# A square on VectorE, a bf16 maximum in a buffer of its own: adaLN block with linear attention and an int8 feed-forward

## The reference

```python
mod = (silu(c) @ wmod).reshape(8, 6, 1, -1)       # sa, ca, ga, sb, cb, gb
ga, gb = (2*(g >= 0) - 1) * max(abs(g), 0.25)     # for both
h = layernorm(x) * (1 + ca) + sa
q, k = relu(h Wq^T) / 8, relu(h Wk^T) / 8         # 16 heads of 64
v, u = h Wv^T, silu(h Wu^T)
out = rms_norm(q @ (k^T v)) * u                   # linear attention, no softmax
x = x + ga * (out Wo^T)
h = layernorm(x) * (1 + cb) + sb
# feed-forward: weight and activations quantised to int8 values
s = max(abs(h), over the 1024 features, at least 1e-8) / 127   # one per token
h_q = clip(round(h / s), -128, 127)
x = x + gb * ((h_q @ w_q^T) * s * w_scale + bias)
```

## Time and profile before

| | us |
|---|---|
| median of 3 runs | 1288.71 |
| lowest and highest | 1287.86, 1291.77 |
| the profiled execution | 1294.28 |
| its span on the slowest core (6) | 1292.0 |
| spans of the 8 cores | 1260.3 to 1292.0 |
| busy on core 6: PE, DVE, ACT, POOL | 609.8, 356.0, 299.3, 65.0 |
| chain that ended last, by engine | PE 42%, DVE 20%, ACT 16%, DMA 14%, issue 7% |

### The profile page before, as it was taken

How to read it: one execution, slowest core, us unless ns; L and a number is a source line. 1 busy time by engine, 2 the same in 40 slices (tenths; PEclk the granted TensorE clock), 3 DMA queues, 4 the chain that set the end, 5 groups by cost and what they waited for, 6 DMA issues and landing times.

```text
span 1292.0 us, 7788 instructions; the slowest of 8 cores (1260.3 to 1292.0 us)
## 1 busy us (share of the span) xinstructions
PE 609.8 (47%) x2360; PEld 241.5 (19%) x2360; DVE 356.0 (28%) x602; ACT 299.3 (23%) x450; POOL 65.0 (5%) x68
## 2 busy tenths in 40 slices
PE   0747565039869498970033421743124621435215
PEld 0101024014324143430010110211111210202102
DVE  0000000750130300002414345142642525424342
ACT  0000000223233332320442123312153023430242
POOL 0010100000000000000000000300002000200003
PEclk9988775569979899995555765756556755757657
DMA  8497751453020000016010100201002010021001
GB/s 197 133 212 173 211 119 20 78 76 54 1 33 1 1 1 1 1 37 158 0 33 0 33 1 0 98 0 33 1 0 98 0 33 0 0 98 33 1 0 65
DMA packets 33332, 65.69 MB, mean 51 GB/s; under 512 B 2437, under 2 KB 14854, under 8 KB 33294
## 3 DMA queue, kind: packets, MB, share of 16 engines
q0 software_dynamic: 17808, 44.04, 15.8%
q1 hardware_dynamic: 15486, 21.16, 4.9%
HBM read 75.69 MB, written 8.39 MB: 65 GB/s over the span
## 4 chain that ended last, share of the span: by engine, by line
PE 42%; DVE 20%; ACT 16%; DMA 14%; issue 7%; SPq 0%; DVEq 0%; ACTq 0%; POOLq 0%; POOL 0%; PEldq 0%
PE pb L67 42%; DMA wmq<-wmod 6%; DVE h L67 3%; DVE x_fma L67 3%; ACT o_bf L67 3%; ACT ouxq L67 2%; DVE ouxq L67 2%; DVE x_fmb L67 2%; DMA fwS<-ffn_w 2%; DMA bias_c<-ffn_b 2%; DVE x L67 2%; DVE xq_i L67 2%; DVE rowsB L67 2%; ACT h L67 2%; DMA x_fmb<-x_fm 2%
## 5 line engine op out<-in xcount | busy, mean ns | idle before, releaser
L67 PE MATMUL pb<-wmq,silc 128*1 128x512 f32 x192 | 98.6, 673 | 88.9 <-DMA wmq<-wmod 50.6
L67 PE MATMUL pb<-ouxq,fqT 128*128 128x512 bf16 x256 | 64.9, 421 | 74.3 <-ACT ouxq L67 74.3
L67 PE MATMUL pb<-ouxq,woT 128*128 128x512 bf16 x256 | 66.5, 428 | 7.0 <-DVE ouxq L67 7.0
L67 DVE COPY mrow<-pb 1x512 f32<-1x512 f32 x12 | 8.1, 679 | 178.4 <-PE pb L67 178.4
L67 ACT ACTIVATE ouxq<-x 128x4096 bf16<-128x4096 f32 x4 | 14.5, 3616 | 175.9 <-DVE x L67 175.9
L67 ACT ACT_TABLE_LOAD x16 | 20.5, 1283 | 142.7 <-POOL amx L67 43.9
L67 DVE TENSOR_REDUCE ws_c<-fwS 128x1 f32<-128x1024 f32 x8 | 9.1, 1214 | 156.9 <-DMA fwS<-ffn_w 156.9
L67 PE MATMUL pb<-id_f,x_fmb 128*128 128x128 f32 x32 | 8.2, 437 | 93.1 <-DVE x_fmb L67 93.1
L67 PE MATMUL pb<-h1a,wqT 128*128 128x512 bf16 x128 | 35.2, 444 | 34.3 <-ACT q_sb L67 34.3
L67 PE MATMUL pb<-ouxq,zc_b 128*1 128x512 bf16 x32 | 13.4, 597 | 80.5 <-ACT o_bf L67 80.5
L67 PE MATMUL pb<-id_b,wqb 128*128 128x128 bf16 x64 | 9.4, 302 | 85.8 <-ACT wqb L67 55.5
(11 more groups left out here) (126 smaller groups left out, 1017.3 us busy)
## 6 DMA issues: line engine op xcount, KB each, us to landing
wmq<-wmod POOLq DMA_DIRECT2D x12, 2048.0 KB, 13.4
x_fmb<-x_fm SPq DMA_DIRECT2D x8, 1024.0 KB, 5.3
out_fm<-h SPq DMA_DIRECT2D x4, 2048.0 KB, 7.3
x_tm<-x_tm POOLq DMA_DIRECT2D x4, 1024.0 KB, 12.9
x_fma<-x_fm POOLq DMA_DIRECT2D x4, 1024.0 KB, 10.9
fwS<-ffn_w SPq DMA_DIRECT2D x1, 4096.0 KB, 26.0
wqT<-wq_t POOLq DMA_DIRECT2D x1, 2048.0 KB, 31.4
wkT<-wk_t POOLq DMA_DIRECT2D x1, 2048.0 KB, 23.8
```

Of the source, the lines that this page charges most:

```text
L67: ins = f(*a, **kw)
```

## The change

- The maximum gets a buffer of its own, `M_sb`, 1 KB per partition in bf16, in a gap ahead of `x2`. The reduction thus writes bf16, and the four transposing matmuls have bf16 on both sides, with `id_b` in place of the f32 identity `id_f`.
- The first load of `x_fmb` in a tile no longer waits for the transposes of the tile before, only for its second residual add.
- The square of the row sums is made by DVE, from the f32 tile `x2` and not from its bf16 copy. It waits for the second residual add, no longer for the cast, and for DVE's own last multiply of step 2.

```diff
-    M_sb = x_fmb
+    M_sb = sb("M_sb", [128, TT], BF16, at=U0 + 13312)
...
             if hf == 0 and i:
-                w.append(f"B{i-1}_mtr")
+                w.append(f"B{i-1}_xa1")
             sch.op("sync", ld(x_fmb[:], dap(dx_fm, i * TT + hf * 256,
                                             [[T, 128], [128 * T, NC], [1, 256]])),
                    waits=w, inc=sXB, event=f"{pe}_xf{hf}", inc_n=16)
...
         def x2sq(e):
-            return e.activation(out=o_bf[:], in_=ouxq[:], func=AF.Square)
-        sch.op("scalar", x2sq, waits=[f"{pe}_x2b"], inc=sS, event=f"{pe}_x2q")
+            return e.tensor_mul(out=o_bf[:], in0=x2[:], in1=x2[:])
+        sch.op("vector", x2sq, waits=[f"{pe}_xa1", f"{pe}_ou{NP-1}"],
+               inc=sV, event=f"{pe}_x2q")
...
                 ins = e.matmul(pb[7][:, g * 128:(g + 1) * 128],
-                               M_sb[:, g * 128:(g + 1) * 128], id_f[:],
+                               M_sb[:, g * 128:(g + 1) * 128], id_b[:],
                                start=True, stop=True)
```

## The result

The changed kernel takes 1266.3 us in the median (10 runs, 1264.0 to 1273.6), the kernel before 1289.4 (10 runs). The ratio is 0.984, 95% interval 0.9814 to 0.9865: 17 to 24 us less, where 19.2 were forecast and the median was forecast at 1269.5. In some executions the cores of one die run longer at a lower clock, as in two of before, above 1320 us; the ratios leave these out and the medians don't, so I take the ratio, 20.6 us, as the gain.

The account below looks back on a forecast made before the run. It took each tile as one chain handed between barely overlapping engines; 13.5 us (square) plus 5.7 (transposes) gave 19.2, so 1288.7 - 19.2 = 1269.5 us, range 1264 to 1278 for 8 in 10.

Parts of the forecast that it names:

- The term of the square: Last residual add to row sums: square on DVE beside ACT's cast, PE starts after 4.66 us, 13.5 us gained.
- The term of the transposes: Between the maximum and its second reduction: four bf16 matmuls take 0.59 us instead of 2.05, 5.7 us gained.
- The maximum at nothing: Large reduction on DVE: writing bf16 while still reading strided stays at 7.03 us, so no gain.
- Its bound of 2.2 us per tile: Large reduction: most it could gain if it reached the contiguous pace, 4 x 1.214 = 4.86 us.
- The load at nothing: First x_fmb load of a tile: its earlier wait gains nothing, as SP's queue holds it behind the store.
- The sum of 19.2 us: Stage B, all four tiles: 13.5 us from the square plus 5.7 us from the transposes.
- Rival 1: Cast and square: DVE and ACT hinder one another reading x2 at once, 4.7 us left, 1284 us; 5 in 100.
- rival 2: Square on DVE runs at the strided reduction's pace, only transposes pay: 8.8 us, 1280 us; 5 in 100.
- rival 4: Large reduction gains from its bf16 output, up to 4 x 2.2 us: 1261 us; 4 in 100.
- Rival 3: Large matmul groups: PE's clock rises later, three groups staying low would give 1303 us; 3 in 100.
- the prediction's own sign: Forecast wrong if the multiply exceeds 5 us, the cast lengthens, or large matmul groups leave 15.5 to 17 us.
- most of 1: Share of rival 1 counted in the 0.94 chance of faster by more; its rest made no difference, 0.03.

Follow-up runs that it names:

- the wait alone: The kernel before with the maximum in its own f32 buffer and the first x_fmb load waiting for the earlier event: ratio 1.0007.
- by_block: The changed kernel plus one whole-tile residual load, adds in the evictions, cast and square per block, row-sum waits reordered: 0.9304 of the kernel before, 1196.2 us.

## Why the prediction was right, point by point

- The term of the square: 13.5 us forecast, 12.6 from the rows; its own experiment gave 13.5 by the ratio and 12.5 in stage B. The multiply was built at 4.41 us and takes 4.43. Mis-sized was the handover to PE: 0.15 from the maximum's row, but 0.36 here, because two waits stand behind the decisive one. With the multiply's 4.43 that makes 0.9 us over four tiles. That a bf16 output costs nothing was read from a multiply whose inputs are bf16 too; it held for f32 inputs.
- The term of the transposes: 5.7 forecast, 5.8 in the profile. The row of the weight preparation held, 0.59 and 0.58 us.
- The maximum at nothing: 7.03 us with either output type. The prediction left open whether the stride or the short runs make it slow; it is the stride. Its bound of 2.2 us per tile for a contiguous pace was too small: four instructions of 1.214 us count their fixed cost four times, and one took 4.42 us, 2.6 less.
- The load at nothing: shown by the wait alone, 0.0 us in stage B.
- The sum of 19.2 us: the rows give 18.4, and the matmul groups took back 1.2 of it, so that stage B fell by 17.6. That the ratio's 20.6 us lie as close is in part luck: some 3 us of them stand ahead of stage B.
- Rival 1 (the engines hinder one another) is excluded by 4424 against 4426 ns, rival 2 by the same rows, rival 4 by the 7034 ns. Rival 3 (the clock rises later) didn't decide. In part it is there: the row sums became longer, by 1.2 us in the mean of the cores, but the large groups did not, and none of them stayed low. By the prediction's own sign, large groups outside 15.5 to 17 us, it would count as wrong, with two of 15.3 us on core 6; but before had one of 15.4 too, and a shorter group is no harm.
- That core 6 should stay the slowest was right in the profile, but no rule: in the experiments it was core 0, 1, 2, 5, 6 or 7.
- One slip in the chances: "most of 1" is 0.02 of rival 1's 0.05 there. Nothing else rests on it.

## What to carry to other kernels

Where engines hand one chain on, a move pays by what it puts side by side and not by a shorter instruction: DVE's square is slower than ACT's (4.43 against 3.62 us), and the change gains only because the cast runs at the same time. Before moving an operation off a chain look for what it could be done beside; with the adds in the evictions, and square and cast block by block behind them, all but the last block's left the chain, and the kernel went from 0.984 to 0.930. A wait that is taken away is worth nothing where the queue's order holds the same instruction back.

## What was not expected of the hardware

- The waits of one operation are instructions of their own, one per semaphore, and are worked through in the order written. The ones behind the decisive one cost about 0.1 us each, fulfilled as they are: 0.46 us with three behind it, 0.36 with two, 0.14 with none.
- Less idle time ahead of a group of matmuls can give back more than itself. After 5.8 to 21 us of idle time the 16 row sums took 4.9 to 6.6 us; where the granted clock was read they began at its lower level, 0.50. After 1.9 us they took 3.61, at 1.00 throughout. No run here lies between 1.9 and 5.8 us. The same code differs by up to 1.7 us per group from tile to tile. Over four tiles and in the mean of the cores the row sums and large groups together differ from those of before by -1.1 to +4.9 us, in kernels where only their surroundings changed, by_block left out. A forecast from the chain's links alone carries that error, up to 0.4%.
